# Who normalises: four tiles per half layer, in VectorE's `stats` entry or in ScalarE's `turn` entry

## The reference

```
def _layernorm(x, axis=-1, eps=1e-05):
    m = jnp.mean(x, axis=axis, keepdims=True)
    v = jnp.var(x, axis=axis, keepdims=True)
    return (x - m) / jnp.sqrt(v + eps)

x = x + attention_i(_layernorm(x), ctx, weights)
x = x + ffn_i(_layernorm(x), weights)
```

## Time and profile before

| | |
|---|---|
| median of 3 runs | 1665.19 us |
| the profiled execution | 1667.29 us |
| its span | 1665.6 us |
| TensorE matmul busy | 84% |
| VectorE busy | 64% |
| ScalarE busy | 28% |
| GpSimd busy | 18% |
| DMA, mean | 58 GB/s |

### The profile page before, as it was taken

One profiled execution on the slowest core, in us unless ns is written; L12 is line 12 of the kernel. 1 busy time (PEld: TensorE's weight loads), 2 busy tenths in 40 slices (PEclk: granted clock), 3 DMA queues, 4 the chain that ended last, 5 costly groups with the idle time before them and its releaser, 6 DMA issues.

```text
span 1665.6 us, 18427 instructions
## 1 busy us (share of the span) xinstructions
PE 1396.8 (84%) x6285; PEld 1072.1 (64%) x6285; DVE 1072.8 (64%) x2413; ACT 459.8 (28%) x993; POOL 294.9 (18%) x170
## 2 busy tenths in 40 slices
PE   6569999999899998979845687669997779688998
PEld 5437776777677767867634466546886546577886
DVE  4656867767777766965797656774447399744141
ACT  3213333232333432313222201312212333322010
POOL 4101111121111112201111102204442221012110
PEclk9779999999999999989976798879999899899999
DMA  6521222213222321122101111200112000011001
GB/s 195 158 76 48 82 75 78 75 57 91 66 66 67 89 71 53 56 77 79 43 11 59 45 42 43 83 18 14 51 48 66 26 13 1 1 38 64 16 25 51
DMA packets 99407, 96.38 MB, mean 58 GB/s; under 512 B 13139, under 2 KB 72419, under 8 KB 99315
## 3 DMA queue, kind: packets, MB, share of 16 engines
q1 hardware_dynamic: 98802, 94.35, 19.4%
q0 software_dynamic: 512, 0.85, 0.2%
HBM read 84.34 MB, written 10.82 MB: 57 GB/s over the span
## 4 chain that ended last, share of the span: by engine, by line
PE 61%; DVE 25%; issue 5%; ACT 3%; DMA 3%; SPq 2%; POOL 1%; ACTq 0%; DVEq 0%; POOLq 0%
PE bank L1663 46%; PE bank L2030 5%; PE bank L1755 4%; DVE nf_y L1608 3%; DVE st L1173 2%; PE bank L1688 2%; DVE xn L1191 1%; SPq L771 1%; PE bank L1745 1%; DVE mx L1224 1%; DVE mx L1525 1%; DMA nf_a<-in_L_w 1%; DVE xT L1150 1%; ACT e L943 1%; DVE sm L1537 1%
## 5 line engine op out<-in xcount | busy, mean ns | idle before, releaser
L1663 PE MATMUL bank<-xT,slots 128*128 128x512 f32 (+1 forms) x1920 | 468.0, 402 | 10.9 <-DVE xT L1150 7.5
L1663 PEld LDWEIGHTS bank<-xT,slots 128*128 128x128 f32 (+1 forms) x1920 | 355.0, 186 | 110.9 <-issue 8.8
L817 POOL TENSOR_TENSOR slots<-staging,slots 128x1024 fp32r<-128x1024 f32 (+4 forms) x97 | 229.4, 2368 | 1081.5 <-ACT slots L910 1081.4
L1608 DVE TENSOR_SCALAR nf_y<-nf_w 128x512 fp32r<-128x512 f32 (+2 forms) x495 | 235.7, 503 | 36.6 <-PE bank L2030 35.4
L1663 PE MATMUL bank<-slots,h 128*128 128x512 f32 (+1 forms) x728 | 180.6, 408 | 20.6 <-DVE h L1280 14.4
L1663 PEld LDWEIGHTS bank<-slots,h 128*128 128x128 f32 (+1 forms) x728 | 141.9, 196 | 56.9 <-DVE h L1280 15.3
L2030 PE MATMUL bank<-nf_y,nf_d 128*128 128x512 f32 (+2 forms) x495 | 165.7, 418 | 14.0 <-DVE nf_y L1608 11.5
L910 ACT ACTIVATE slots<-staging 128x1024 fp32r<-128x1024 f32 (+4 forms) x97 | 98.2, 1019 | 185.0 <-PE bank L1663 172.6
L943 ACT ACTIVATE e<-bank,mx 128x320 f32<-128x320 f32 x128 | 66.3, 523 | 267.1 <-DVE mx L1227 253.6
L2030 PEld LDWEIGHTS bank<-nf_y,nf_d 128*128 128x128 f32 (+1 forms) x495 | 93.4, 193 | 52.1 <-DVE nf_y L1608 19.7
L1755 PE MATMUL bank<-eT,v 128*96 128x256 f32 (+1 forms) x384 | 112.6, 416 | 1.1 <-ACT eT L953 1.1
(11 more groups left out here) (249 smaller groups left out, 1790.2 us busy)
## 6 DMA issues: line engine op xcount, KB each, us to landing
staging<-in_L_wqkT SPq DMA_DIRECT2D x16, 480.0 KB, 3.6
nf_out<-nf_w SPq DMA_DIRECT2D x30, 256.0 KB, 2.1
staging<-nf_out SPq DMA_DIRECT2D x30, 256.0 KB, 2.8
staging<-in_L_woT SPq DMA_DIRECT2D x16, 384.0 KB, 3.6
staging<-in_L_w SPq DMA_DIRECT2D x12, 512.0 KB, 3.7
nf_a<-nf_max SPq DMA_DIRECT2D x40, 128.0 KB, 3.4
nf_r<-nf_rcp SPq DMA_DIRECT2D x40, 128.0 KB, 3.5
nf_w<-in_L_w SPq DMA_DIRECT2D x15, 256.0 KB, 4.3
```

The costliest lines, as they stand in the source:

```text
L817: g.tensor_tensor(lo, split_source(i), hi.bitcast(FP32), ALU.subtract).then_inc(*sig.mark("weight_low", i))
L1608: v.tensor_scalar(nf_y[0:rows, i % STAIR_RING, 0:size], w_, bound, first, compare, ALU.mult)\
L1663: ins = mm(dst, l_, r_, start=i == 0, stop=i == len(passes) - 1)
```

## The change

VectorE's `stats` no longer writes the normalised tiles. It ends with one small product, `mr`, minus the mean times `rs`, for the four tiles at once, and signals `scales_ready`. ScalarE's `turn` entry now begins with the four tiles: an Identity activation with scale `rs` and bias `mr`, each one value per partition. The wait for the transposes of the half before moves with it. The sum of |xn| in layer 5 moves from VectorE's `stats` to the head of VectorE's `turn`, behind a wait for the last normalised tile, and in (5,1) and (6,0) ScalarE waits for the sum before it overwrites `xn`. The list of entries is as before.

```diff
+        mr = sb("mr", [P, TILES], FP32)
...
             def turn(layer, hf):
+
+                act.wait_ge(*sig.when("scales_ready", (layer, hf)))
+                if layer or hf:
+                    act.wait_ge(*sig.when("turn_product", (layer, 0, KT - 1) if hf else (layer - 1, 1, KT - 1)))
+                if layer == 5 and hf or layer == 6 and not hf:
+                    act.wait_ge(*sig.when("strength", 0 if hf else 1))
+                for t in range(hf * TPH, (hf + 1) * TPH):
+                    sc.activation(xn[:, t % TPH], x[:, t], ACT.Identity, scale=rs[:, t:t + 1], bias=mr[:, t:t + 1])\
+                        .then_inc(*sig.mark("normalised", (layer, t)))
                 for c in range(KT):
...
-                if layer or hf:
-                    prev = (layer, 0, KT - 1) if hf else (layer - 1, 1, KT - 1)
-                    dve.wait_ge(*sig.when("turn_product", prev))
-                for t in ts:
-                    v.tensor_scalar(xn[:, t % TPH], x[:, t], mv[:, t, 0:1], rs[:, t:t + 1], ALU.subtract, ALU.mult)\
-                        .then_inc(*sig.mark("normalised", (layer, t)))
+                v.scalar_tensor_tensor(mr[:, sl], mv[:, sl, 0], -1.0, rs[:, sl], ALU.mult, ALU.mult)\
+                    .then_inc(*sig.mark("scales_ready", (layer, hf)))
+
+            def turn(layer, hf):
                 if layer == 5:
-                    dve.wait_ge(*sig.when("normalised", (layer, ts[-1])))
-                    v.tensor_reduce(ab[:, sl], xn[:], AX.X, ALU.add, apply_absolute_value=True)\
+                    dve.wait_ge(*sig.when("normalised", (layer, hf * TPH + TPH - 1)))
+                    v.tensor_reduce(ab[:, hf * TPH:(hf + 1) * TPH], xn[:], AX.X, ALU.add, apply_absolute_value=True)\
                         .then_inc(*sig.mark("strength", hf))
-
-            def turn(layer, hf):
                 for c in range(KT):
```

## The result

The changed kernel takes 1674.53 us (median of 4 runs, 1672.24 to 1676.86), the kernel before in the same session 1665.21 (1661.99 to 1666.86): ratio 1.0058, 95% interval 1.0036 to 1.0081, or +9.7 us. The prediction said 1676. The profiled execution took 1676.86 us with a span of 1674.9; by the terms of the sum it should have been 1678.4.

The account below looks back on a forecast made before the run. TensorE, 84% busy, sets the time where it is fed and waits elsewhere, notably for xn and xT. Prices 28.7 less gains 17.55 gave +11.1 us on a median of 1665.19: 1676 us, range 1664 to 1685, forecast's chance 0.64.

Parts of the forecast that it names:

- (b): Five places where xn was long ready when TensorE came and ScalarE had just taken the product before: +11.75 us.
- (a): Four places where TensorE already waits for xn and ScalarE is free: +3.85 us.
- (c): Four places where ScalarE's queue holds a link waiting for VectorE ahead of turn: +11.85 us.
- Gains: VectorE's stats entries 1.7 us shorter at nine awaited places, plus 2.25 for a moved reduction: 17.55 us saved.
- Prices: Delays from ScalarE normalising at turn, summed over four kinds of place: +28.7 us.
- (d): Three covered places, layers 2, 3 and 5, half 0, where passes lie beneath other work: +1.25 us.
- (1,0): Layer 1, half 0, a (b) place: ScalarE's copies start later, but VectorE came later still; +1.8 us.
- (4,0): Layer 4, half 0, a (b) place: copies start at 1049.2 instead of 1046.54; +2.7 us.
- (7,0): Layer 7, half 0, a (b) place: ScalarE 2.9 us later, VectorE 2.0 behind; +2.4 us.
- clock rival: TensorE's clock falls in new gaps at four (b) places, 1.7 us each: 6.8 us more, 1683 us; chance 0.17.
- Absorbed: VectorE is the bound behind each (b) place, so those delays don't last: 1664.5 us, no change; chance 0.11.
- Faster: ScalarE waits at turn before TensorE arrives, so normalising is covered in (b) and (c): 1660.5 us; chance 0.08.

Follow-up runs that it names:

- rebuilt: The changed kernel's sixteen groups on ScalarE at the head of turn, rewritten in the variants' common frame with 45 more semaphore waits: 1672.69 us, ratio 1.0044 to the kernel before.
- the covered three: Kernel before with only layers 2, 3 and 5, half 0, normalised on ScalarE at turn, layer 5's sum at VectorE's turn: 1654.92 us, ratio 0.9945.
- the control: The variants' frame with nothing moved to ScalarE, every engine's instructions as in the kernel before: 1661.06 us, ratio 0.9986 to the kernel before.
- (b) at turn: Kernel before with only the five (b) places normalised on ScalarE, at the head of its turn entry: 1668.26 us, ratio 1.0030.
- VectorE at turn: Kernel before with all sixteen groups kept on VectorE but moved, with the sums of |xn|, to the head of its turn entry: 1669.57 us, ratio 1.0035.
- shorter passes: Changed kernel with the activation reading no bias, so the mean is not taken off: 1663.27 us, ratio 0.9983 to the kernel before.
- (b) early: Kernel before with the five (b) places on ScalarE, tile by tile earlier in its queue than turn: 1644.90 us, ratio 0.9883.
- their two halves: Kernel before with part of the five places early on ScalarE: layers 0 and 1, 1656.11 us, ratio 0.9948; layers 4, 6 and 7, 1652.75 us, ratio 0.9930.

## Why the prediction was right

The time and the sign were right, +9.7 (+7.3 in the rebuilt one) where the sum said +11.1, and so was the mechanism in most of the 16 places. That the total came so near is partly luck: falls of the clock made the prices 4.9 us dearer than forecast, and 4.7 us came back where the forecast had nothing. And the places don't simply add up: of the four kinds run alone, (b) gave +5.0 for a forecast of +3.3 and the covered three -9.2 for -5.9, but (a) gave +0.5 for +3.85 and (c) -1.7 for +10. By its steps:

**Passes.** 2.9 us for four, measured 2.92 with 0.80 each. No table load came with them: ScalarE has seven in both traces. The run without the bias shows that their length counts (-10.2 us, give or take 4, for 0.37 us less in each of 14 places, 5.2 us).

**Gains.** Forecast 17.55, measured 19.5. (6,0) gave 2.9 instead of 1.7, (4,1) 2.4.

**Prices.** Forecast 28.7, measured 33.6. Kinds (a), (c) and (d) came within 0.5 us each in the changed kernel, and (0,1) and (6,0) as worked out. Three terms of (b) were too small: 3.1 for 1.8 at (1,0), 3.8 for 2.7 at (4,0) and 5.3 for 2.4 at (7,0). At (1,0) and (7,0) it is the clock rival's event, and at (4,0) slow transposes too, as the table below shows. At (1,0) the transposes took 1.1 us and the six products behind them 0.6 us longer than at full clock, which is more than the missing 1.3.

**Between the places.** Minus 4.7 us came where the change touches nothing; I had put this at 0 without a reason. This is what hid the error of the prices. That it is low-clock time wasn't read piece by piece, and the control, with nothing changed, is 2.3 us ahead of before at its end too.

**The clock rival** named four places and 6.8 us. How long the 13 last transposes of a turn took, in us, from one profile each:

| | (0,1) | (1,0) | (4,0) | (7,0) |
|---|---|---|---|---|
| before | 1.58 | 1.58 | 1.77 | 1.63 |
| changed kernel | 1.64 | 2.73 | 3.03 | 3.04 |
| rebuilt | 1.64 | 2.92 | 3.03 | 3.04 |
| (b) at turn | 1.64 | 2.95 | 3.03 | 3.04 |
| VectorE at turn | 1.64 | 3.03 | 2.20 | 3.03 |
| shorter passes | 1.64 | 1.64 | 3.04 | 3.03 |
| (b) early | 1.58 | 1.58 | 2.25 | 1.58 |

So new falls come at (1,0) and (7,0), with either engine at the head of turn, and go when the passes stand early. With passes of 0.70 us the fall at (1,0) is gone too. At (4,0) the clock fell before too:
```profile
1045.44 2.40 PE L1688 MATMUL bank<-ident,xn 128*128 128x128 f32 x16
```
In the changed kernel it has fallen by 1049.8 us, in the products ahead of the new gap, so the gap isn't shown to be its cause. The Trainium skill (TensorE: Matmul & The Clock Gate, "HAM oscillation") says that idle gaps bring half the clock back. (7,0), with a gap of 2.19 us, agrees. At (1,0) the clock falls with gaps of only 0.32 and 0.38 us, and (0,1), with 0.80, 0.31 and 0.38, shows no fall: the length of the gap alone doesn't decide it here. What the three places cost beyond the forecast, 1.3, 1.1 and 2.9, is 5.3 us, and three times the rival's 1.7 is 5.1. As a sum, too, the rival was nearer than its chance: all of the extra time in the changed kernel's profile is busy time at low clock, 9.5 us, and its idle time is unchanged. The forecast's steps are partly this (slow transposes at (4,0), (4,1), (7,0)), so it and the rival aren't as apart as I wrote them.

**Absorbed** is refuted for (b), by its steps, by the +5.0 of its own run where this rival said -8, and by the passes' length counting. For (c) alone a delay was absorbed, at (3,1) by the clock and not by VectorE. **Faster** is refuted for the change, but its condition is confirmed: with ScalarE's passes ahead of the transposes the price goes away, and the (b) places give -19.5 instead of +5.0. Its price for them, 0.6 each, was too cautious.

**Open.** Why the early versions gain up to 10 us beyond their steps, and why the (a) and (c) places alone cost next to nothing. At (3,1) it is a low-clock stretch that vanishes; for the five early places the mean clock of all executions gives some 9 to 11 of the 19.5 us, and for their two halves it gives little. No run here controls where the clock falls far from the edit. That a shift of one stage decides where it falls later was argued from the traces, not shown by an experiment of its own.

## What to carry to other kernels

When an operation moves to an idle engine, look where it lands in that engine's queue before its price: the same passes at the head of `turn` lose 5 us and a few entries earlier win 19.5. Move it into the entries in which the consumer isn't waiting yet, and only at the places where the old engine's next result is awaited. And split every difference into the matmul engine's idle time and its busy time: if the busy time moves while the matmuls are the same, the clock is in it, local steps won't add up, and a change of under half a per cent can't be read from one profile: single profiled executions lay up to 0.5% off the median of their kernel here. The mean clock of all executions is the better witness.

## What was not expected of the hardware

- Identical instructions gave two profiles that differ by 2.0 us near the start and by 3.3 us, the other way, between 265 and 341 us.
- A delay of 3.5 us in front of a product was paid back within 54 us: the product then ran at clock 1.00 instead of 0.50 and took 2.92 us instead of 5.35.
- Gaps of 0.32 and 0.38 us between transposes at (1,0) go with a fall of the clock in the changed kernel; with gaps of 0.22 and 0.28, in the run with shorter passes, there is none.
- The same instructions of ScalarE in another place of its queue moved TensorE's busy time by 25.9 us and its idle time by 4.4 in the profiles; over all executions it is an estimated 19 and 5.
